# Slot attention in one kernel: the inverse root in two parts, low halves, maxima, new slots and tanh moved

## What is computed

```python
Pn = rmsnorm(P, input_norm_w)
k_proj = Pn @ Wk.T
v_proj = Pn @ Wv.T
for _ in range(3):
    sn = rmsnorm(slots, slot_norm_w)      # slots * rsqrt(mean(slots^2) + eps) * w
    q_proj = sn @ Wq.T
    scores = einsum('bkd,bmd->bkm', q_proj, k_proj) * SCALE
    attn = softmax(scores, axis=-2)       # over the 56 slots
    attn = attn / (sum(attn, axis=-1) + EPS)
    updates = einsum('bkm,bmd->bkd', attn, v_proj)
    slots = gru_cell(updates, slots, ...)
# gru_cell: r, z = sigmoid(..), n = tanh(xn + r * hn), slots = (1 - z) * n + z * h
```

## Time and profile before

| | us |
|---|---|
| median of three runs | 823.46 |
| lowest and highest | 821.6, 823.87 |
| profiled execution, its own time | 828.05 |
| its span, first to last instruction | 826.3 |
| slot iterations in it | 462 to about 690 |

### The profile page before, as it was taken

The page is one execution under the profiler, slowest core; times in us unless marked ns, Lnnn a source line. Parts: engine busy times, 40 slices in busy tenths (PEclk is TensorE's granted clock), DMA queues, the critical chain, the costliest instruction groups (busy, mean ns, idle before and its releaser), DMA issues.

```text
span 826.3 us, 24071 instructions
## 1 busy us (share of the span) xinstructions
PE 697.6 (84%) x8999; PEld 498.9 (60%) x8999; DVE 589.1 (71%) x1092; ACT 537.1 (65%) x1164; POOL 415.1 (50%) x492
## 2 busy tenths in 40 slices
PE   5777999999999999997805688888788885899997
PEld 2255777777777777775402478777677783344443
DVE  4975788887888888887786667677777655566663
ACT  3354677777777777765452698789988872455554
POOL 1859577777777777700000135444445430466664
PEclk8898999999999999999856979899988896899999
DMA  6315544444444444230400405432540440212100
GB/s 198 106 38 164 143 126 133 131 130 132 129 132 129 131 130 132 66 71 8 183 0 25 207 2 176 173 119 79 205 184 3 155 155 2 75 39 77 38 1 23
DMA packets 26545, 85.75 MB, mean 104 GB/s; under 512 B 5780, under 2 KB 7316, under 8 KB 26468
## 3 DMA queue, kind: packets, MB, share of 16 engines
q1 hardware_dynamic: 26472, 84.77, 32.5%
HBM read 65.46 MB, written 0.46 MB: 80 GB/s over the span
## 4 chain that ended last, share of the span: by engine, by line
PE 51%; DVE 15%; POOL 12%; ACT 9%; issue 7%; SPq 3%; DMA 2%; POOLq 0%; DVEq 0%; ACTq 0%
POOL ctx_lo L601 8%; PE ps L1341 8%; PE ps L1358 7%; PE ps L1372 7%; PE ps L1605 5%; ACT c_prob L766 4%; PE ps L1328 4%; PE ps L1589 3%; PE ps L1317 2%; PE ps L1377 2%; ACT w0T L766 2%; SPq L439 2%; DVE tile_max L853 1%; PE ps L1623 1%; DVE amax_part L1077 1%
## 5 line engine op out<-in xcount | busy, mean ns | idle before, releaser
L853 DVE TENSOR_REDUCE tile_max<-ps 128x1 f32<-128x500 f32 x336 | 214.7, 674 | 52.0 <-PE ps L1341 51.2
L627 ACT ACTIVATE probs<-ps 125x896 f32<-125x896 f32 x192 | 175.3, 916 | 95.5 <-PE ps L1358 94.5
L1341 PE MATMUL ps<-k_hi,qdiag 128*128 128x500 f16 x336 | 130.4, 390 | 7.7 <-DVE tile_max L853 6.5
L766 ACT ACTIVATE c_prob<-ps,c_bias,row_scale 125x56 f32<-125x56 f32 x384 | 116.1, 479 | 3.0 <-DVE c_bias L1164 2.7
L578 POOL TENSOR_TENSOR c_prob<-c_prob,c_weight 125x672 f32<-125x672 f32 x32 | 41.9, 1312 | 133.7 <-DVE c_weight L1178 133.7
L1358 PE MATMUL ps<-qstack,kstack 98*125 98x224 f16 x768 | 107.1, 263 | 0.4
L601 POOL TENSOR_TENSOR ctx_lo<-ctx_hi,ctx_lo 128x448 f16<-128x448 f32 x64 | 71.9, 1124 | 70.5 <-ACT ctx_lo L811 70.5
L1358 PEld LDWEIGHTS ps<-qstack,kstack 98*125 98x125 f16 x768 | 86.6, 137 | 21.3 <-ACT probs L627 2.8
L1372 PE MATMUL ps<-probs,v_aug 125*32 125x168 f32 x1536 | 75.4, 314 | 3.3 <-ACT probs L627 2.5
L1659 PE MATMUL ps<-ctx_lo 128*128 128x448 f16 x192 | 68.5, 357 | 6.6 <-DVE ctx_hi L1276 2.8
L534 POOL TENSOR_TENSOR rows_in<-rows_in 125x768 f32<-125x768 f32 (+2 forms) x96 | 68.8, 717 | 7.5
(11 more groups left out here) (264 smaller groups left out, 1706.3 us busy)
## 6 DMA issues: line engine op xcount, KB each, us to landing
row_tiles<-in_ctx_rows_wide SPq DMA_DIRECT2D x40, 774.0 KB, 5.7
ctx<-in_ctxT SPq DMA_DIRECT2D x16, 750.0 KB, 5.4
rows_in<-in_ctx_rows SPq DMA_DIRECT2D x16, 750.0 KB
kstack<-k_hi SPq DMA_DIRECT2D x128, 93.8 KB, 3.2
kstack<-k_lo SPq DMA_DIRECT2D x64, 93.8 KB, 3.1
ctx_hi<-in_wg SPq DMA_DIRECT2D x8, 256.0 KB, 2.7
ctx_hi<-in_wu SPq DMA_DIRECT2D x8, 256.0 KB, 3.0
ctx_hi<-in_wd SPq DMA_DIRECT2D x8, 256.0 KB, 3.4
```

Source lines behind the costliest of these rows:

```text
L627: nc.scalar.activation(probs[c % RING_P][0:CH, :].rearrange("p (k w) -> p k w", k=2), score_tile(c)[0:CH], ACT.Exp, scale=float(HD) ** -0. ...
L766: last = nc.scalar.activation(c_prob[n % PROBS][:, c, :], ps[0:CH, 2 * (n % 2) + c // 6, bass.ts(c % 6, TOK)], ACT.Exp, bias=c_bias[n % 2] ...
L853: nc.vector.reduce_max(tile_max[:, u % MAXT, u // MAXT:u // MAXT + 1], ps[:, MAXB + (u + p) % 2, 0:KCOLS], AX.X).then_inc(max_done, 1)
L1341: nc.tensor.matmul(ps[:, MAXB + (u + p) % 2, 0:KCOLS], qdiag[p][:, bass.ts(t, 128)], k_hi[p][:, bass.ts(j, KCOLS)], start=True, stop=True) ...
```

## The change

The root works on 224 columns. `slot_means` is one product with a full matrix of 1/128, so that each partition gets the mean of each of the 224 slots of the group, and `project_slots` moves into it, on slots that are not yet scaled. `spread_roots` and `normed_slots` are gone; `scaled_queries` multiplies the projected queries in PSUM by the root. The three Newton steps become one Newton step and one step of higher order, issued as two parts with one unit's multiplication between them. The maxima `c_max` lie in PSUM. The offsets of the tables change, and with them the order of the steps that share a slot. The diff, cut to its core:

```diff
@@ -204,7 +204,7 @@
-        c_max = [sbuf(f"c_max{i}", [CH, NCH], stack=sc) for i in range(2)]
+        c_max = [ps[0:CH, 2 * i, GW + 128:GW + 128 + NCH] for i in range(2)]
...
@@ -215,9 +215,9 @@
-        rs_var = sbuf("rs_var", [128, TOK], stack=sc)
-        rs_y = sbuf("rs_y", [128, TOK], stack=sc)
-        rs_a = sbuf("rs_a", [128, TOK], stack=sc)
+        rs_var = sbuf("rs_var", [128, QT], stack=sc)
+        rs_y = sbuf("rs_y", [128, QT], stack=sc)
+        rs_a = sbuf("rs_a", [128, QT], stack=sc)
...
@@ -314,10 +313,10 @@
-        TENSOR_AT = dict(spread=55, project=59, sums=(19, 27), turn=31, gates=39, means=47)
-        SCALAR_AT = dict(copy=28, tanh=36, cand=39, hi=54)
-        VECTOR_AT = dict(rows=27, hidden=39, slots=41, root=45, normed=53, lo=57)
-        POOL_AT = dict(root=40)
+        TENSOR_AT = dict(sums=(19, 27), turn=35, gates=39, means=51)
+        SCALAR_AT = dict(copy=31, tanh=38, cand=41, hi=57)
+        VECTOR_AT = dict(rows=27, hidden=41, slots=45, root=49, scaled=57, lo=58)
+        POOL_AT = dict(root=(44, 48))
...
@@ -342,6 +341,7 @@
+        means, projected = (ps[:, QUERY, bass.ts(i, QT)] for i in range(2))
...
@@ -581,17 +581,30 @@
             def inverse_root(g):
                 pool.wait_ge(r_guess, g + 1)
-                for i in range(3):
-                    wait(pool, r_inv, 3 * g + i)
-                    nc.gpsimd.tensor_tensor(rs_a[:], rs_y[:], rs_y[:], ALU.mult).then_inc(r_step, 1)
-                    pool.wait_ge(r_step, 9 * g + 3 * i + 1)
-                    nc.gpsimd.tensor_tensor(rs_a[:], rs_a[:], rs_var[:], ALU.mult).then_inc(r_step, 1)
-                    pool.wait_ge(r_step, 9 * g + 3 * i + 2)
-                    nc.gpsimd.tensor_scalar(rs_a[:], rs_a[:], -0.5, 1.5, ALU.mult, ALU.add).then_inc(r_step, 1)
-                    pool.wait_ge(r_step, 9 * g + 3 * i + 3)
-                    nc.gpsimd.tensor_tensor(rs_y[:], rs_y[:], rs_a[:], ALU.mult).then_inc(r_inv, 1)
-
-            iterations(unit, [(POOL_AT["root"], True, inverse_root)])
+                nc.gpsimd.tensor_tensor(rs_a[:], rs_y[:], rs_y[:], ALU.mult).then_inc(r_step, 1)
+                pool.wait_ge(r_step, 8 * g + 1)
+                nc.gpsimd.tensor_tensor(rs_a[:], rs_a[:], rs_var[:], ALU.mult).then_inc(r_step, 1)
+                pool.wait_ge(r_step, 8 * g + 2)
+                nc.gpsimd.tensor_scalar(rs_a[:], rs_a[:], -0.5, 1.5, ALU.mult, ALU.add).then_inc(r_step, 1)
+                pool.wait_ge(r_step, 8 * g + 3)
+                nc.gpsimd.tensor_tensor(rs_y[:], rs_y[:], rs_a[:], ALU.mult).then_inc(r_inv, 1)
+
+            def second_root(g):
+
+                pool.wait_ge(r_inv, 2 * g + 1)
+                nc.gpsimd.tensor_tensor(rs_a[:], rs_y[:], rs_y[:], ALU.mult).then_inc(r_step, 1)
+                pool.wait_ge(r_step, 8 * g + 4)
+                nc.gpsimd.tensor_tensor(rs_var[:], rs_a[:], rs_var[:], ALU.mult).then_inc(r_step, 1)
+                pool.wait_ge(r_step, 8 * g + 5)
+                nc.gpsimd.tensor_scalar(rs_a[:], rs_var[:], 0.375, -1.25, ALU.mult, ALU.add).then_inc(r_step, 1)
+                pool.wait_ge(r_step, 8 * g + 6)
+                nc.gpsimd.tensor_tensor(rs_a[:], rs_a[:], rs_var[:], ALU.mult).then_inc(r_step, 1)
+                pool.wait_ge(r_step, 8 * g + 7)
+                nc.gpsimd.tensor_scalar(rs_a[:], rs_a[:], 1.875, None, ALU.add).then_inc(r_step, 1)
+                pool.wait_ge(r_step, 8 * g + 8)
+                nc.gpsimd.tensor_tensor(rs_y[:], rs_y[:], rs_a[:], ALU.mult).then_inc(r_inv, 1)
+
+            iterations(unit, [(POOL_AT["root"][0], True, inverse_root), (POOL_AT["root"][1], True, second_root)])
             for u in range(UNITS_F):
...
@@ -788,9 +801,8 @@
-                act.wait_ge(qc_ready, g + 1)
-                nc.scalar.activation(query_hi[:, quad(g)], ps[:, QUERY, 288:288 + QT], ACT.Copy,
-                                     scale=norm_w[:, 1:2]).then_inc(qc_hi, 1)
+                act.wait_ge(r_slots, g + 1)
+                nc.scalar.activation(query_hi[:, quad(g)], projected, ACT.Copy, scale=norm_w[:, 1:2]).then_inc(qc_hi, 1)
...
@@ -1158,10 +1170,10 @@
-                nc.vector.tensor_reduce(c_max[i][:].rearrange("p (k c) -> p k c", k=2), wide, AX.X, ALU.max).then_inc(c_maxed, 1)
+                nc.vector.tensor_reduce(c_max[i].rearrange("p (k c) -> p k c", k=2), wide, AX.X, ALU.max).then_inc(c_maxed, 1)
-                nc.vector.scalar_tensor_tensor(out=c_bias[i][:], in0=c_max[i][:], scalar=-1.0, in1=row_scale[:, n % BATCH, :],
+                nc.vector.scalar_tensor_tensor(out=c_bias[i][:], in0=c_max[i], scalar=-1.0, in1=row_scale[:, n % BATCH, :],
...
@@ -1227,24 +1239,23 @@
             def root_guess(g):
                 dve.wait_ge(r_var, g + 1)
-                wait(dve, r_inv, 3 * g)
-                wait(dve, r_spread, g)
-                step(nc.vector.tensor_scalar(rs_var[:], ps[:, QUERY, 0:TOK], RMS_EPS, None, ALU.add), r_var_eps, g + 1)
+                wait(dve, r_inv, 2 * g)
+                wait(dve, r_slots, g)
+                step(nc.vector.tensor_scalar(rs_var[:], means, RMS_EPS, None, ALU.add), r_var_eps, g + 1)
                 nc.vector.tensor_scalar(rs_y[:].bitcast(I32), rs_var[:].bitcast(I32), -0.5, ROOT_GUESS, ALU.mult, ALU.add).then_inc(r_guess, 1)
-            def normed_slots(g):
-                dve.wait_ge(r_spread, g + 1)
-                wait(dve, qc_ready, g)
-                nc.vector.tensor_tensor(slots_n, slots_of(g), ps[:, QUERY, 64:64 + QT], ALU.mult).then_inc(r_slots, 1)
+            def scaled_queries(g):
+                dve.wait_ge(r_inv, 2 * g + 2)
+                nc.vector.tensor_tensor(projected, projected, rs_y[:], ALU.mult).then_inc(r_slots, 1)
             def query_low(g):
                 dve.wait_ge(qc_hi, g + 1)
-                nc.vector.scalar_tensor_tensor(out=query_lo[:, quad(g)], in0=ps[:, QUERY, 288:288 + QT], scalar=norm_w[:, 1:2], in1=query_hi[:, quad(g)],
+                nc.vector.scalar_tensor_tensor(out=query_lo[:, quad(g)], in0=projected, scalar=norm_w[:, 1:2], in1=query_hi[:, quad(g)],
                                                op0=ALU.mult, op1=ALU.subtract).then_inc(qc_done, 1)
             iterations(unit, [
-                (VECTOR_AT["rows"], False, update_rows), (VECTOR_AT["hidden"], False, hidden_part), (VECTOR_AT["slots"], False, new_slots),
-                (VECTOR_AT["slots"], True, slot_squares), (VECTOR_AT["root"], True, root_guess), (VECTOR_AT["normed"], True, normed_slots),
+                (VECTOR_AT["rows"], False, update_rows), (VECTOR_AT["scaled"], True, scaled_queries), (VECTOR_AT["hidden"], False, hidden_part),
+                (VECTOR_AT["slots"], False, new_slots), (VECTOR_AT["slots"], True, slot_squares), (VECTOR_AT["root"], True, root_guess),
                 (VECTOR_AT["lo"], True, query_low)], before_drain=lambda: weights(UNITS_C - 1))
             def weights_high(e):
...
@@ -1628,26 +1639,12 @@
             def slot_means(g):
                 pe.wait_ge(r_sq, g + 1)
                 wait(pe, qc_done, g)
-                for i in range(QUAD):
-                    last = nc.tensor.matmul(ps[32 * i:32 * i + 32, QUERY, 0:TOK], ones_mean[:, 0:32], rms_sq[:, bass.ts(i, TOK)], start=True, stop=True)
-                last.then_inc(r_var, 1)
-
-            def spread_roots(g):
-                pe.wait_ge(r_inv, 3 * g + 3)
-                wait(pe, r_slots, g)
-                for i in range(QUAD):
-                    last = nc.tensor.matmul(ps[:, QUERY, 64 + TOK * i:64 + TOK * (i + 1)], spread[:, i, :], rs_y[:], start=True, stop=True)
-                last.then_inc(r_spread, 1)
-
-            def project_slots(g):
-                pe.wait_ge(r_slots, g + 1)
-                wait(pe, qc_done, g)
-                nc.tensor.matmul(ps[:, QUERY, 288:288 + QT], to_query[:], slots_n, start=True, stop=True).then_inc(qc_ready, 1)
+                nc.tensor.matmul(means, ones_mean[:], rms_sq, start=True, stop=True)
+                nc.tensor.matmul(projected, to_query[:], stream[:, quad(g)], start=True, stop=True).then_inc(r_var, 1)
             iterations(unit, [
-                (TENSOR_AT["spread"], True, spread_roots), (TENSOR_AT["project"], True, project_slots),
-                (TENSOR_AT["sums"][0], False, update_sums(0)), (TENSOR_AT["sums"][1], False, update_sums(1)),
-                (TENSOR_AT["turn"], False, turn_updates), (TENSOR_AT["gates"], False, gate_sums), (TENSOR_AT["means"], True, slot_means)])
+                (TENSOR_AT["means"], True, slot_means), (TENSOR_AT["turn"], False, turn_updates), (TENSOR_AT["gates"], False, gate_sums),
+                (TENSOR_AT["sums"][0], False, update_sums(0)), (TENSOR_AT["sums"][1], False, update_sums(1))])
             pe.wait_ge(x3_done, 1)
...
```

More of the change, by code:

```diff
@@ L229, in build @@
         rms_sq = in_work(9, 1)
-        slots_n = in_work(10, 1)
         first_sd_rows = in_work(10, 1)
@@ L289, in build @@
             sem(n) for n in ("gates_ready", "tanh_done", "g_step", "cand_ready", "cand_done", "slots_done"))
```

(4 more changed lines are left out.)

## The result

The changed kernel takes 819.8 us (median of six executions, 818.1 to 821.1), the kernel before 823.7 in the same series; the ratio is 0.9958, between 0.9938 and 0.9978. The change saves 3.9 us, 0.4%. The direction was right and the time lies inside the wide range of 804 to 820.5, but outside the forecast's own 810 to 818, and the saving was forecast two and a half times too large (9.6 us).

What follows compares the result with a forecast made beforehand. A loop through the engines bounds the slot iterations, no engine being full. Savings of 8.2 between units 9 and 45, 1.5 ahead and 0 after, together 9.6 to 9.7 us, give 814 us; own range 810 to 818, wide range 804 to 820.5.

Steps and rivals of the forecast that it cites:

- the base of the sum: Nine periods from unit 9 to unit 45: 156.1 us against 164.3 in the profiled execution before, 8.2 saved.
- After unit 45 the order on TensorE is nearly the same ...: 0, within 1: End of the slot iterations, after unit 45: last multiplication, update sums, gates and slots still in sequence; 0 us saved, within 1.
- ahead of unit 9: Start of the slot iterations: a 1.77 us wait goes, but transposes and update sums come before the scores; 1.5 us saved.
- the root's loop: Loop from scaled_queries through VectorE (9.6 us) and GpSimd (7.8), 0.1 handing over: 17.5 us, independent of TensorE's clock.
- the sum: Whole kernel: 8.2 us saved between units 9 and 45, 1.5 ahead, 0 after; together 9.6 to 9.7.
- The period of 17.5: Slot iterations: each of the last eight periods takes 17.5 us, set by the loop through GpSimd's root.
- rival 2: Slot iterations: the low clock holds TensorE's loop, period 17.8 to 18.2, time 816 to 820 us; chance 0.17.
- The loop of 16.1 us through TensorE: Slot iterations: the chain through TensorE and VectorE sums to 16.1 us per group at full clock.
- Waits: Slot iterations: L782's and the transposes' waits go, 2.0 plus 1.2 us per period; TensorE's pause moves before first-unit scores.
- Two low stretches in a row: TensorE's clock in the slot iterations: in each group, TensorE's loop grows 3.4 to 19.5, time 830 us; rival's chance 0.06.
- Maxima in PSUM: VectorE's 48 reductions and 48 small instructions: priced at nothing, bounds 0.03 us either way each, 1 us in all.
- The rule of the Trainium skill that the prediction weighed: VectorE's 48 small instructions: fixed part 120 cycles with PSUM source against 58 with SBUF, 65 ns more each; 815 us.

Runs made afterwards that it cites:

- a_root: The changed kernel with the root's ninth instruction (L603) written as multiply by 1.0 and add 1.875 instead of one add: 813.6 us, 0.9882 of before.
- a_fill: The changed kernel plus ten idle 128x512 products on TensorE behind the scores of each group's last unit: 815.6 us, 0.9913 of before.
- a_fill_root: The changed kernel with ten idle products and the root's ninth instruction as multiply and add: 812.0 us, 0.9851 of before.
- a_swap_fill: The changed kernel with ten idle products and the reset part (hidden_part) ahead of scaled_queries on VectorE: 804.7 us, 0.9769 of before.
- b_maxps: The kernel before with only the maxima moved to PSUM: 824.3 us, 1.0001 of before.
- a_maxsb: The changed kernel with the maxima back in SBUF: 823.4 us, 0.9993 of before.
- b_again1: The kernel before, unchanged, profiled and timed again: 825.3 us in the profiled execution, timed median 822.8.
- b_fill: The kernel before plus eight idle 128x512 products on TensorE ahead of the transposes of groups 0 to 9: 813.7 us, 0.9889 of before.

## Why the prediction was right in direction and wrong in size

**The steps that failed** are two. The first is the base of the sum: "156.1, against 164.3: 8.2 saved", and with it "The median of the shown runs is 823.46, 4.6 lower, so 813.9". The 164.3 were one execution's; four traces have 164.3, 161.0, 160.9 and 163.9, in the mean 162.5, so that 156.3 found for the changed kernel is 6.2 less and not 8.2. The forecast took the saving against the longest of the four and then subtracted it from a median that such an execution lies 4.4 us above (828.05 against 823.66), while that of the changed kernel lies 1.1 below its own (818.75 against 819.8). The second is "After unit 45 the order on TensorE is nearly the same ...: 0, within 1", with nothing put down for what follows the stage: 1.9 us were lost after unit 45 and 1.0 behind the stage, in both traces of the changed kernel. In a_root's trace, with the same order, it was 0.2 and 0.1, so they come with where low stretches fall and not with the new work. With 1.7 saved ahead of unit 9 the traces give 1.7 + 6.2 - 1.9 - 1.0 = 5.0 us, and the timed medians 3.9 and 4.6.

The cause of the first is the clock. With one engine order, the period of before was 17.3, about 18.5 or about 19.6, by whether a low stretch fell into it and how long it was. The changed kernel has a low stretch in every period, but each at a place where the root's loop is nearly as long; its two traces differ by 0.1 in the nine. Of the 4.4 us between the profiled execution and the median, the traces put 2.0 in the slot iterations (228.6 against 226.6 in the mean of four). Where the rest lies stays open: the three other profiled executions are also 1.3 to 1.9 us above the median, and timed executions have no trace.

**Luck in the first two traces.** Between them alone the sum seems to hold: 9.6 to 9.7 forecast, 9.3 found. From unit 9 to unit 45 it was 156.1 forecast and 156.2 found, 8.0 less; ahead of unit 9 1.5 forecast and 2.2 found. After unit 45 2.0 were lost, the last period being 10.31 with TensorE at 0.59 of its clock in the 4 us from 672 on, against 8.63 in a_root. Behind the stage 1.0 more was lost (136.7 against 135.7), and 2.2 were won ahead of it (the first score at 459.8 instead of 462.0), where the change does nothing. The sum of these, 2.2 + 8.0 - 2.0 - 1.0 + 2.2 = 9.4, came near the forecast's because the errors cancel: the 2.2 ahead of the stage are luck.

**The period of 17.5** was right for a partly wrong reason. The root took 6.7 us (forecast 6.4; L603, counted at 0.38, took 0.78), the multiplication beside it 1.4, the guesses 0.7 (forecast 0.95). But VectorE waited for the root only four times, 1.7 us in all, not 1 to 1.5 us in each group; the chain shows both loops joined, with the scores at 1.86. That is the forecast's rival 2 standing level with the forecast: 17.5 and 17.8 were too near each other to be two cases. At full clock the wait for the root is there as forecast, up to 1.4 us in a_fill and 1.0 in a_fill_root. The loop of 16.1 us through TensorE is seen where the clock is held and the root is off the end: 16.1 to 16.4 in a_swap_fill.

**Waits.** That L782's and the transposes' waits go, that TensorE's pause moves to the scores (forecast 3.8 us in one piece, found up to 3.2) and that a low stretch follows it in nearly every group was right. Two low stretches in a row, a sign of being wrong by the prediction, came once in nine periods, at 608 us, and cost 1.7 us.

**Maxima in PSUM** were costed at nothing, within 1 us; they are worth 3.6 to 4.8. The step looked at VectorE's own duration by memory and not at who else uses SBUF then. The old order's trace had seven held instructions (L1164, up to 0.62 us), which cost no time there (b_maxps); in the new places of GpSimd's work there are 22. The Trainium skill, GPSIMD Engine Reference, section "8. Key points", says that GpSimd's SBUF interfaces are shared with VectorE and that they contend when VectorE reads two inputs from SBUF. The rows of L1176 agree (378 against 171 ns). The rule of the Trainium skill that the prediction weighed, a larger fixed part for a PSUM source, is not borne out here: L1176 took 171 ns with its input in PSUM, and 170 at the least with both in SBUF.

## What to carry to other kernels

Where a loop's period depends on whether the clock fell, one profiled execution is a draw: read the same stage in several traces, take savings from their mean, and leave out what differs ahead of the stage. An execution that lies off the timed median is a warning to do this before any term is taken as a saving. Before an order is rewritten to hide a TensorE pause, fill the pause with idle products: here eight of them gave 10 us, the new order 4, and the new order with idle products and one more swap 19. Where GpSimd gets more work, look for small VectorE instructions with two SBUF inputs beside it and give one of them a PSUM input.

## What the runs showed of the hardware that was not expected

A VectorE instruction of 125 x 12 elements with two SBUF inputs took up to 1.21 us while GpSimd multiplied in SBUF, and ended with it (a_maxsb); 0.17 us with one input in PSUM. On GpSimd a tensor_scalar of 128 x 224 with an addition alone took 782 ns, with a multiplication by one ahead of it 378. And matmuls whose result is thrown away shortened the kernel by 10 us: over 500 to 650 us the granted clock was 0.93 in b_again1 and 1.00 with them (b_fill).
